# A stack of four cross-attention layers: output product in rounded halves, operands in fewer buffers, another order of jobs

## The chip, the core and the metric

The kernel runs on one core of a Trainium2 chip. The metric is the device time of one execution in microseconds (us), as the median of several runs. Five engines work side by side, each through its own instructions in order: TensorE (PE, its weight loads shown as PEld), VectorE (DVE), ScalarE (ACT), GpSimd (POOL) and SyncE (SP, which here only issues transfers). They meet through semaphores. TensorE writes to eight accumulation banks (PSUM) of 512 fp32 columns each.

## What is computed

Sixteen batches of x (100 rows by 256) go through four layers against a context of 361 rows by 256 each. The two narrow layers (L0 first, L3 last) have 16 heads of width 16; L0 ends in a feed-forward part of width 1024. The two wide layers (L1, L2) have 16 heads of width 64, so their queries, keys and values are 1024 wide. The wide part, cut to what matters:

```python
q = split_heads(norm(x) @ wq)        # 256 -> 16 heads of 64
k, v = split_heads(ctx @ wk), split_heads(ctx @ wv)
if layer == "L2": q, k = rope(q), rope(k)
attn = softmax(q @ k.T)
x = x + (attn @ v).reshape(100, 1024) @ wo     # the O product
if layer == "L2": x = layer_norm(x)
```

Everything is fp32.

## The kernel before

`build` runs four blocks, one after the other, each with a program for every engine and a barrier between: `narrow_layer("L0")`, `feed_forward`, `wide_layers` (L1 for the 16 batches, then L2 for the same 16: 32 sequences s, NS = 32, B = 16), `narrow_layer("L3")`.

**Rounded halves.** Most products do not multiply fp32 by fp32. Each operand is split in a high half (ACT copies it to the type f32r, which rounds) and a low half (DVE takes source minus high half), and `product3` (L1316) issues for each pair of operands three matmuls, high x high, high x low, low x high, into one bank. Exceptions in the wide layers are the transposes, the product with V and the **O product** (`project`, L1370 to L1381): eight fp32 matmuls of 100 weight columns by 256 columns. The trace shows an fp32 matmul that is no transpose as two rows.

**Wide layers.** A sequence is worked in four slots d = 0 to 3, each with two pairs of heads. `jobs_at(s, d)` (L1192) lists the side jobs of a slot, in three groups; every engine walks the same lists. A job takes one of three banks in turn (`begin`), and so waits until the third job before it has been taken out of its bank (`taken`). Jobs are: K, two per slot, for the next sequence; V, six per sequence (0 to 5), each 128 or 105 context rows by 512; Q and X (queries and the transpose of x, for two sequences together); R, twice per sequence, which spreads the inverse softmax sums of eight heads over partitions; O, once. TensorE's slot is: two `scores`, two `weigh` of the slot before, the jobs `first` (K, K), `turn` (six transposes), the jobs `mid` (R, V, O), `turn`, the jobs `late` (Q, X).

In L2 the keys and queries are rotated as well: DVE shuffles the result in its bank (`shuffle`, L1622), ACT then copies it out (`copy_turn`, L1482), which frees the bank, POOL multiplies (`rotate`, L1856, L1857), DVE adds (`join`, L1627), ACT rounds (L1490), DVE (K, L1633) or POOL (Q, L1863) makes the low half. For each sequence of L2 POOL also makes tables from the mask (L1837 to L1841). The scores get one matmul pair more (L1398).

After the weighing of eight heads, ACT copies R's result to OT (`spread`, L1513), DVE multiplies it by the weighed sums (`scale`, L1682) and so frees the bank PO for the next eight heads; O follows when both halves of OT are there, and DVE adds its result to X (`finish`, L1688).

**Contexts** come from memory through one raw buffer C and are split into three slots (s % 3) of CTH2 and CTL2, at d = 1, two sequences ahead (L1469, L1609). **Weights** come through W_RAW, three buffers of 1 MB; 15 chunks are split (`split_high` L1461, `split_low` L1604). SP's order at the start of the wide layers:

```python
load_output_weights(sp, "L1")
...
sp.wait_ge(Z["w_low"], 7)
load_weights(sp, "L2")
for s in range(NS):
    if s + 1 < NS:
        sp.wait_ge(Z["c_low"], KE * (s + 1))
        load_turned_context(sp, s + 1)
```

The L2 chunks are split at the ends of slots in sequences 13 to 15 (`CHUNKS_AT`), after the jobs `late`. The closing norm of L2 (`post_stats`, `post`) stands at the ends of d = 2 and d = 3.

**Narrow layers.** Before the slots stands a list FIRST: W jobs (biases, 16 matmuls of one column each, twice), context turns, K, X, Q, V. K's strips go out to memory and come back in another layout (`strips`) before scores can use them. Matmul rows with these lines: L369 (K, Q), L394 (W), L424 (V), L509 (scores), L521 (`turn`).

## Time and profile before

| | us |
|---|---|
| median of 3 runs (lowest, highest) | 2072.18 (2070.36, 2076.41) |
| profiled execution, its own time | 2078.45 |
| its span in the trace | 2076.5 |
| PE busy | 1940.1 (93%) |
| PEld busy | 1669.4 (80%) |
| DVE busy | 1383.3 (67%) |
| ACT busy | 1290.3 (62%) |
| POOL busy | 602.2 (29%) |
| mean granted TensorE clock | 0.975 |

The profiled execution has 2.0 us outside its span and is 6.3 us above the median of the runs. Reading the trace by stages: L0 runs until about 357 us, the feed-forward part until 448, L1 until about 1092, L2 until 1740, L3 until the end. Busy shares are averages over these stages, and they differ from one to the next; matmuls are pipelined and their ends are modelled, so what one costs is read from start to start. A clock of 1.00 is 2.4 GHz and one of 0.50 is 1.2 GHz.

### The profile page before, as it was taken

How to read it: one execution, taken by the hardware profiler on the slowest of the kernel's cores; microseconds unless marked ns; L12 is line 12 of the kernel's file. 1: busy time of each engine (PE TensorE's matmuls, PEld its weight loads, DVE VectorE, ACT ScalarE, POOL GpSimd, SP SyncE). 2: the span in 40 equal slices, each digit the busy share in tenths (PEclk: the TensorE clock that was granted, in tenths of full speed). 3: DMA queues.
4: the chain of work that ended last, by engine and by line, in shares of the span. 5: the costliest groups of instructions: out<-in, count | busy, mean ns of one | idle time of the engine just before them, and what ended most of it. 6: DMA issues, size and time to landing. Idle time of an engine off the chain costs nothing. (4 is left out here: it accounts for less than half of the span.)

```text
span 2076.5 us, 49737 instructions
## 1 busy us (share of the span) xinstructions
PE 1940.1 (93%) x18664; PEld 1669.4 (80%) x18664; DVE 1383.3 (67%) x2711; ACT 1290.3 (62%) x3125; POOL 602.2 (29%) x740
## 2 busy tenths in 40 slices
PE   6899997988999999999999999999999998899997
PEld 5777775986888888888888888888888877777776
DVE  5777875554555545555577888888878874677774
ACT  3677775655556555555666666666666653677775
POOL 3223230000000000000047766866776751000000
PEclk9999998999999999999999999999999998999998
DMA  5544442102000000000001000000000001434441
GB/s 163 154 129 141 135 127 80 62 23 83 8 16 9 10 14 8 16 9 9 15 2 52 10 16 10 10 13 14 10 10 17 2 1 54 124 114 130 128 130 54
DMA packets 72853, 109.56 MB, mean 53 GB/s; under 512 B 7052, under 2 KB 62508, under 8 KB 72620
## 3 DMA queue, kind: packets, MB, share of 16 engines
q1 hardware_dynamic: 72332, 105.88, 16.9%
q8 instruction: 154, 2.52, 0.5%
q14 instruction: 79, 0.65, 0.1%
q10 hardware_dynamic: 288, 0.51, 0.1%
HBM read 69.18 MB, written 37.19 MB: 51 GB/s over the span
## 5 line engine op out<-in xcount | busy, mean ns | idle before, releaser
L1533 ACT ACTIVATE wide_P<-PS,MX 100x361 f32<-100x361 f32 x512 | 280.8, 562 | 178.6 <-DVE MX L1660 178.6
L623 ACT ACTIVATE L_P<-PS,MX 100x361 f32<-100x361 f32 x512 | 252.7, 565 | 121.5 <-DVE MX L753 121.3
L753 DVE TENSOR_REDUCE MX<-PS 100x2 f32<-100x722 f32 x256 | 219.9, 901 | 49.3 <-PE PS L509 49.0
L1660 DVE TENSOR_REDUCE MX<-PS 100x2 f32<-100x722 f32 x256 | 221.3, 901 | 26.7 <-PE PS L1401 26.3
L521 PE MATMUL PP<-CON,L_P 100*128 100x100 f32 x1536 | 185.9, 259 | 25.8 <-DVE L_PT L760 17.0
L521 PEld LDWEIGHTS PP<-CON,L_P 100*128 100x128 f32 x1536 | 153.2, 145 | 47.7 <-ACT L_P L623 33.4
L1408 PEld LDWEIGHTS PS<-CON,wide_P 100*128 100x128 f32 x1536 | 159.7, 140 | 24.1 <-ACT wide_P L1533 3.0
L1408 PE MATMUL PS<-CON,wide_P 100*128 100x100 f32 x1536 | 175.5, 249 | 1.4 <-ACT wide_P L1533 1.2
L1856 POOL TENSOR_TENSOR wide_AC<-wide_T,wide_COSM 128x362 f32<-128x362 f32 x128 | 130.0, 1016 | 154.2 <-ACT wide_T L1482 148.6
L1507 ACT ACTIVATE wide_V<-PJ 128x512 f32<-128x512 f32 (+1 forms) x126 | 75.3, 598 | 145.2 <-PE PJ L1321 143.3
L1421 PEld LDWEIGHTS PP<-wide_PT,wide_V 128*64 128x64 f32 (+1 forms) x3072 | 136.0, 136 | 32.5 <-issue 32.5
L1421 PE MATMUL PP<-wide_PT,wide_V 128*64 128x100 f32 (+1 forms) x3072 | 161.2, 253 | 0.1
L1816 POOL TENSOR_TENSOR VE<-MV 128x2 f32<-128x2 f32 x8 | 1.7, 218 | 505.8 <-DVE MV L1713 505.8
L1321 PE MATMUL PJ<-wide_CTH,wide_WH 128*128 128x362 f32 x336 | 120.7, 359 | 15.6 <-DVE wide_CTL L1609 9.5
L1857 POOL TENSOR_TENSOR wide_SH<-wide_SH,wide_SINM 128x362 f32<-128x362 f32 x128 | 132.5, 1036 | 0.0
L1321 PE MATMUL PJ<-wide_WH,wide_CTH 128*128 128x512 f32 (+1 forms) x252 | 107.5, 427 | 12.1 <-ACT wide_T L1482 11.2
L1321 PE MATMUL PJ<-wide_CTH,wide_WL 128*128 128x362 f32 x336 | 111.5, 332 | 0.0
L1321 PE MATMUL PJ<-wide_CTL,wide_WH 128*128 128x362 f32 x336 | 111.3, 331 | 0.0
L760 DVE COPY L_PT<-PP 128x600 f32<-128x600 f32 x128 | 99.5, 777 | 13.4 <-PE PP L521 9.0
L1533 ACT ACTIVATION_READ_ACCUMULATOR wide_P<-PS,MX 100x1 f32 x512 | 103.8, 203 | 0.0
L1633 DVE TENSOR_TENSOR wide_KL<-wide_AC,wide_KH 128x362 fp32r<-128x362 f32 x128 | 102.9, 844 | 0.0
L1666 DVE COPY wide_PT<-PS 128x600 f32<-128x600 f32 x128 | 99.1, 774 | 2.3 <-PE PS L1408 2.3
(242 smaller groups left out, 5369.5 us busy)
## 6 DMA issues: line engine op xcount, KB each, us to landing
strips<-L_KS SPq DMA_DIRECT2D x256, 90.5 KB
L_KA<-strips SPq DMA_DIRECT2D x64, 362.0 KB, 3.1
C<-ctx_t SPq DMA_DIRECT2D x32, 361.0 KB, 3.1
kept<-L_CTH SPq DMA_DIRECT2D x16, 361.0 KB, 4.6
kept<-L_CTL SPq DMA_DIRECT2D x16, 361.0 KB, 5.5
L_CTH<-kept SPq DMA_DIRECT2D x16, 361.0 KB, 4.2
L_CTL<-kept SPq DMA_DIRECT2D x16, 361.0 KB, 5.2
C<-in_ctx SPq DMA_DIRECT2D x8, 256.0 KB, 3.4
```

Of the source, the lines that this page charges most:

```text
L521: last = nc.tensor.transpose(PPB[:, n, SQ * t:SQ * t + SQ], P[:, (4 * g + 2 * i + n) % 8, 128 * t:128 * t + 128], ident[0:SQ, 0:SQ])
L623: nc.scalar.activation(P[:, (4 * g + j) % 8, 0:SK], PSB[0:SQ, j, 0:SK], ACT.Exp, bias=MX[:, s % 2, 4 * q + j:4 * q + j + 1], scale=1.0).th ...
L753: nc.vector.tensor_reduce(MX[:, s % 2, 4 * q + 2 * i:4 * q + 2 * i + 2], PSB[0:SQ, 2 * i:2 * i + 2, 0:SK], AX.X, ALU.max, negate=True).the ...
L760: nc.vector.tensor_copy(pt(g)[:, 2 * KV_TILES * SQ:4 * KV_TILES * SQ].rearrange("p (n c) -> p n c", n=2), PPB[:, :, 0:KV_TILES * SQ]).then ...
L1321: last = nc.tensor.matmul(dst, l, r, start=n == 0, stop=n == len(todo) - 1)
L1408: last = nc.tensor.transpose(score_bank(g, i)[:, SQ * t:SQ * t + SQ], P[:, (2 * g + i) % 4, 128 * t:128 * t + 128], ident[0:SQ, 0:SQ])
L1421: last = nc.tensor.matmul(PO[64 * i:64 * i + 64, SQ * at:SQ * at + SQ], V[0:r, 1024 * c + 64 * h:1024 * c + 64 * h + 64], PT[0:r, (2 * g + ...
L1533: nc.scalar.activation(P[:, (2 * g + i) % 4, 0:SK], score_bank(g, i)[0:SQ, 0:SK], ACT.Exp, bias=MX[:, s % 2, h:h + 1], scale=1.0, accum_ou ...
L1633: nc.vector.tensor_tensor(KL[:, p, :], AC[:, r % NB, 0:SKE], KH[:, p, :].bitcast(fp32), ALU.subtract).then_inc(Z["k_low"], 1)
L1660: nc.vector.tensor_reduce(MX[:, s % 2, 2 * p:2 * p + 2], PSB[0:SQ, 2 * (g % 2):2 * (g % 2) + 2, 0:SK], AX.X, ALU.max, negate=True).then_in ...
L1856: nc.gpsimd.tensor_tensor(ac, src, c, ALU.mult)
L1857: nc.gpsimd.tensor_tensor(sh, sh, t, ALU.mult).then_inc(Z["rotated"], 1)
```

## The change

1. **O product.** `project` becomes a `product3` over eight pairs: 24 f32r matmuls instead of 8 fp32 ones. OT gives way to a buffer RB of half its size and the halves OTH and OTL. ACT rounds RB (`output_high`, at the ends of d = 2 and of the next d = 0), DVE subtracts (`output_low`, in d = 3 and the next d = 1, behind the maxima): 64 new instructions on each. The weights are split too (`output_weights_high`, `_low`): four chunks of 1024 columns, two of them in L1's slot (0, 1), one each in (16, 3) and (17, 0).
2. **Space.** Contexts in two slots (s % 2), split at d = 3 instead of d = 1. W_RAW has two buffers; a third and WO lie in `shared`, which is given back before the wide layers, where WOL and WOH take its place.
3. **Loads.** SP loads the context of sequence 1 ahead of the L2 weights; Wq and Wv of L2 come then, Wk at s = 14.
4. **Order in the wide layers.** V before R in d = 0 and d = 2; V(s + 1, 0) moves from d = 2 to d = 3. Chunks are split ahead of `mid` instead of behind `late`. `post_stats` and `post` move to d = 1, the latter by a whole sequence.
5. **Order in the narrow layers.** FIRST has K, X, K before the second W; K(1, 0) moves into slot (0, 0).
6. **Fillers.** `keep_busy` issues fp32 matmuls of 128 columns whose result nobody reads: 12 in FIRST of L0, 4 in each of the six slots from (15, 1) to (16, 2) of both narrow layers, 9 at L0's end, 12, 7 and 8 in the feed-forward part, 9 at the start and 4 and 14 at the end of the wide layers.

The diff, cut to its core (indices of DVE's and ACT's job lists that follow FIRST, and s % 3 to s % 2 in the readers, are left out):

```diff
-        W_RAW = sb("W_RAW", [128, 3, 2048])
-        WO = sb("WO", [128, 2048])
+        W_RAW = sb("W_RAW", [128, 2, 2048])
...
+        def keep_busy(dst, n):
+
+            for _ in range(n):
+                nc.tensor.matmul(dst[:, 0:128], ident, CON[:, 0:128], start=True, stop=True)
+
...
+        shared = ExitStack()
+        WO = shared.enter_context(nc.sbuf_tensor("WO", [128, 2048], fp32))
+        W_RAW_Q = shared.enter_context(nc.sbuf_tensor("W_RAW_Q", [128, 2048], fp32))
+
         def raw(c, n):
-            return W_RAW[:, c, 0:KE * n].rearrange("p (k n) -> p k n", k=KE)
+            if c == 2:
+                at = W_RAW[:, 1, 1024:1024 + KE * n] if n == E else W_RAW_Q[:, 0:KE * n]
+            else:
+                at = W_RAW[:, c, 0:KE * n]
+            return at.rearrange("p (k n) -> p k n", k=KE)
...
+                    if s == 0:
+                        b_.append(("K", 1, 0))
...
-            FIRST = ([("W", 0, 0)] + ctx0 + [("W", 0, 1), ("K", 0, 0), ("K", 0, 1), ("X", 0, 0)] + [("Q", 0, t) for t in range(4)]
-                     + [("V", 0, 0), ("V", 0, 1)] + ctx1 + [("K", 1, 0)])
-            lead = len(ctx0) + 5
+            FIRST = ([("W", 0, 0)] + ctx0 + [("K", 0, 0), ("X", 0, 0), ("K", 0, 1), ("W", 0, 1)] + [("Q", 0, t) for t in range(4)]
+                     + ctx1 + [("V", 0, 0), ("V", 0, 1)])
...
                     strips(0, 0)
-                    strips(0, 1)
                     if first:
                         sp.wait_ge(Z["c_normed"], 2)
                         load_context(sp, 3, CS[1], s_c[1])
+                    strips(0, 1)
+                    if first:
+                        keep(0)
                     strips(1, 0)
                     if first:
-                        keep(0)
                         keep(1)
...
-                    for key in FIRST:
+                        keep_busy(PSB[:, 3, :], 6)
+                    for n, key in enumerate(FIRST):
                         job(key)
+                        if first and n in (0, KE):
+                            keep_busy(PSB[:, 3, :], 4 if n == 0 else 2)
...
+                        if (B - 1, 1) <= (s, q) <= (B, 2):
+                            keep_busy(begin(("P" if q == 0 else jobs_at(s, q + 1)[0][0][0], s - 1, 0) if q < 3 else ("O", s - 1, 0)), 4)
+                    keep_busy(PSB[:, 3, :], 9 if first else 0)
...
+                    keep_busy(PSB[:, 3, :], 12)
                     for k in range(KE):
                         turn(0, k)
+                    keep_busy(PSB[:, 3, :], 7)
...
+                    keep_busy(PSB[:, 3, :], 8)
...
+            WOL, WOH = local("WOL", [128, 2048], f32r), local("WOH", [128, 2048], f32r)
             WH, WL = local("WH", [128, 6144], f32r), local("WL", [128, 6144], f32r)
-            CTH2, CTL2 = local("CTH", [128, 3, KE, SKE], f32r), local("CTL", [128, 3, KE, SKE], f32r)
...
-            OT = local("OT", [128, 8, SQ])
+            RB = local("RB", [128, 4, SQ])
+            OTH, OTL = local("OTH", [128, 8, SQ], f32r), local("OTL", [128, 8, SQ], f32r)
+            WO_HALVES = [slice(1024 * n, 1024 * n + 1024) for n in range(2)]
+            WO_AT = {(0, 1): [0, 1], (B, 3): [2], (B + 1, 0): [3]}
             Y = XN[:, 0, :]
...
+                if d == 0 and 0 < s < NS:
+                    mid.append(("V", s, 2))
                 if d == 0 and s > 0:
                     mid.append(("R", s - 1, 1))
-                if d == 0 and 0 < s < NS:
-                    mid.append(("V", s, 2))
                 if d == 1 and s > 0:
                     mid.append(("O", s - 1, 0))
+                if d < 3 and s < NS:
+                    mid.append(("V", s, 3 + d))
                 if d == 2 and s < NS:
                     mid.append(("R", s, 0))
-                if d < 3 and s < NS:
-                    mid.append(("V", s, 3 + d))
-                if d >= 2 and s + 1 < NS:
-                    mid.append(("V", s + 1, d - 2))
+                if d == 3 and s + 1 < NS:
+                    mid += [("V", s + 1, 0), ("V", s + 1, 1)]
...
+                    def weights(m):
+                        sp.dma_start(W_RAW[:, RAW2[m], :].rearrange("p (k n) -> p k n", k=KE),
+                                     a["L2_xattn_W" + m.lower()].rearrange("(k p) n -> p k n", p=128)).then_inc(w_in["L2"]["KVQ".index(m)], 16)
+
                     load_output_weights(sp, "L1")
                     sp.wait_ge(Z["padded"], 1)
                     mask(B)
                     mask(B + 1)
-                    sp.wait_ge(Z["w_low"], 7)
-                    load_weights(sp, "L2")
                     for s in range(NS):
                         if s + 1 < NS:
                             sp.wait_ge(Z["c_low"], KE * (s + 1))
                             load_turned_context(sp, s + 1)
+                        if s == 0:
+                            sp.wait_ge(Z["w_low"], 7)
+                            for m in "QV":
+                                weights(m)
+                        if s == B - 2:
+                            sp.wait_ge(Z["w_low"], 9)
+                            weights("K")
...
-                        pe.wait_ge(Z["scaled"], 2 * (s + 1))
-                        if s == 0:
-                            pe.wait_ge(wo_in["L1"], 16)
-                        if s == B:
-                            pe.wait_ge(wo2_in, 16)
-                        dst = begin(key)
-                        for t in range(8):
-                            last = nc.tensor.matmul(dst[0:SQ, 0:E], OT[:, t, :], WO[:, E * t:E * t + E], start=t == 0, stop=t == 7)
-                        last.then_inc(Z["made"], 1)
+                        pe.wait_ge(Z["o_low"], 2 * (s + 1))
+                        pe.wait_ge(Z["wo_low"], 2 if s < B else 4)
+                        product3(begin(key)[0:SQ, 0:E], [(OTH[:, t, :], OTL[:, t, :], WOH[:, E * t:E * t + E], WOL[:, E * t:E * t + E]) for t in range(8)])
...
+                    keep_busy(PSB[:, 0, :], 9)
                     pe.wait_ge(Z["padded"], 1)
...
+                        if s == NS:
+                            keep_busy(PSB[:, 0, :], 4 if d == 0 else 14)
...
-                            if s >= 3:
-                                act.wait_ge(Z["made"], job_no["V", s - 3, 5] + 1)
-                        nc.scalar.activation(CTH2[:, s % 3, k, 0:SK], ctx_raw(s)[:, k, :], ACT.Copy).then_inc(Z["c_high"], 1)
+                            if s >= 2:
+                                act.wait_ge(Z["made"], job_no["V", s - 2, 5] + 1)
+                        nc.scalar.activation(CTH2[:, s % 2, k, 0:SK], ctx_raw(s)[:, k, :], ACT.Copy).then_inc(Z["c_high"], 1)
...
+                        if 2 * s + r:
+                            act.wait_ge(Z["o_low"], 2 * s + r)
+                        nc.scalar.activation(RB[:, :, :].rearrange("p t q -> p (t q)"), bank(key)[:, 0:4 * SQ], ACT.Copy).then_inc(Z["spread"], 1)
+
+                    def output_high(s, r):
+                        act.wait_ge(Z["scaled"], 2 * s + r + 1)
+                        if s:
+                            act.wait_ge(Z["made"], job_no["O", s - 1, 0] + 1)
+                        nc.scalar.activation(OTH[:, 4 * r:4 * r + 4, :], RB[:, :, :], ACT.Copy).then_inc(Z["o_high"], 1)
+
+                    def output_weights_high(n):
+                        if n < 2:
+                            act.wait_ge(wo_in["L1"], 16)
+                            act.wait_ge(Z["w_low"], 7)
+                        else:
+                            act.wait_ge(wo2_in, 16)
+                            act.wait_ge(Z["made"], job_no["O", B - 1, 0] + 1)
+                        h = WO_HALVES[n % 2]
+                        nc.scalar.activation(WOH[:, h], WO[:, h], ACT.Copy).then_inc(Z["wo_high"], 1)
...
-                        if d == 1 and s + 2 < NS:
+                        if d == 3 and s + 2 < NS:
                             for k in range(KE):
                                 context_high(s + 2, k)
+                        for c in CHUNKS_AT.get((s, d), ()):
+                            split_high(c)
+                        for n in WO_AT.get((s, d), ()):
+                            output_weights_high(n)
                         for key in mid:
                             job(key)
                         if s < NS:
                             unload(2 * G + 1)
                         for key in late:
                             job(key)
-                        for c in CHUNKS_AT.get((s, d), ()):
-                            split_high(c)
+                        if d == 0 and s:
+                            output_high(s - 1, 1)
+                        if d == 2 and s < NS:
+                            output_high(s, 0)
...
-                        o = OT[:, 4 * r:4 * r + 4, :].rearrange("p t q -> p (t q)")
+                        o = RB[:, :, :].rearrange("p t q -> p (t q)")
                         nc.vector.tensor_tensor(o, PO[:, 0:4 * SQ], o, ALU.mult).then_inc(Z["scaled"], 1)
+
+                    def output_low(s, r):
+                        dve.wait_ge(Z["o_high"], 2 * s + r + 1)
+                        t = slice(4 * r, 4 * r + 4)
+                        nc.vector.tensor_tensor(OTL[:, t, :], RB[:, :, :], OTH[:, t, :].bitcast(fp32), ALU.subtract).then_inc(Z["o_low"], 1)
+
+                    def output_weights_low(n):
+                        dve.wait_ge(Z["wo_high"], n + 1)
+                        h = WO_HALVES[n % 2]
+                        nc.vector.tensor_tensor(WOL[:, h], WO[:, h], WOH[:, h].bitcast(fp32), ALU.subtract).then_inc(Z["wo_low"], 1)
...
+                        if d == 1 and s:
+                            output_low(s - 1, 1)
+                        if d == 3 and s < NS:
+                            output_low(s, 0)
...
-                        if d == 1 and s + 2 < NS:
+                        if d == 1 and B + 2 <= s <= NS:
+                            post(s - 2)
+                        if d == 3 and s + 2 < NS:
                             for k in range(KE):
                                 context_low(s + 2, k)
+                        for c in CHUNKS_AT.get((s, d), ()):
+                            split_low(c)
+                        for n in WO_AT.get((s, d), ()):
+                            output_weights_low(n)
                         for key in mid:
                             job(key)
...
-                        if B < s < NS:
-                            if d == 2:
-                                post_stats(s - 1)
-                            if d == 3:
-                                post(s - 1)
+                        if B < s < NS and d == 1:
+                            post_stats(s - 1)
...
+                shared.close()
                 wide_layers()
+                WO = sb("WO3", [128, KE * E])
```

## Rows read from the trace of the kernel before

**Rows 1.** Stages: us, busy time of each engine (instructions), granted clock, DMA share, GB/s
```profile
357.00:371.00 14.00, 6.25 (x23) 5.93 (x24) 10.58 (x22) 7.84 (x9) 2.16 (x2) 0.51 0.74 266
440.00:520.00 80.00, 62.75 (x468) 56.28 (x466) 41.64 (x87) 41.25 (x98) 3.64 (x8) 0.89 0.20 68
560.00:1010.00 450.00, 448.87 (x3850) 390.40 (x3850) 228.65 (x428) 257.82 (x693) 6.61 (x20) 1.00 0.04 11
1136.00:1662.00 526.00, 510.70 (x4440) 444.81 (x4439) 432.85 (x902) 337.56 (x916) 378.66 (x442) 1.00 0.04 11
1740.00:1785.00 45.00, 36.52 (x205) 32.51 (x206) 23.02 (x47) 19.28 (x40) 4.33 (x10) 0.70 0.37 114
```

**Rows 2.** TensorE's waits: who waited for whom, us in total, times, longest
```profile
PE PJ L1321 <- ACT wide_T L1482: 11.2, 10, 1.5
PE PJ L1321 <- DVE wide_CTL L1609: 9.5, 1, 9.5
```

**Rows 3.** Timeline of TensorE, starts of sequences 2, 14, 17 and 30 (start, duration)
```profile
556.03 0.41 PE L1401 MATMUL PS<-wide_KH,wide_QH 64*100 64x362 f32 x2
...
1012.16 0.41 PE L1401 MATMUL PS<-wide_KH,wide_QH 64*100 64x362 f32 x2
...
1135.95 0.41 PE L1398 MATMUL PS<-wide_MNEG,wide_FILL 64*100 64x362 f32 x2
...
1662.81 0.41 PE L1398 MATMUL PS<-wide_MNEG,wide_FILL 64*100 64x362 f32 x2
```

**Rows 4.** Timeline of TensorE: an O product and what follows; f32r matmuls of 256 columns
```profile
570.54 3.62 PE L1380 MATMUL PJ<-WO,wide_OT 128*100 128x256 f32 x16
573.81 0.58 PE L1321 MATMUL PJ<-wide_WH,wide_CTH 128*128 128x512 f32 x1
574.23 0.40 PE L1321 MATMUL PJ<-wide_WL,wide_CTH 128*128 128x512 f32 x1
574.47 0.39 PE L1321 MATMUL PJ<-wide_WH,wide_CTL 128*128 128x512 f32 x1
...
321.11 0.28 PE L424 MATMUL PJ<-L_WH,L_CTH 128*128 128x256 f32 x1
321.23 0.28 PE L424 MATMUL PJ<-L_WL,L_CTH 128*128 128x256 f32 x1
```

**Rows 5.** Timeline of TensorE in L2: the same 512-column job at either clock, and a stall
```profile
1101.05 0.69 PE L1321 MATMUL PP<-wide_WH,wide_CTH 128*105 128x512 f32 x1 [1.69 <-ACT wide_T L1482]
1101.54 0.63 PE L1321 MATMUL PP<-wide_WL,wide_CTH 128*105 128x512 f32 x1
1101.96 0.63 PE L1321 MATMUL PP<-wide_WH,wide_CTL 128*105 128x512 f32 x1
...
1075.76 0.41 PE L1321 MATMUL PJ<-wide_CTH,wide_WH 128*128 128x362 f32 x1 [1.49 <-issue]
```

**Rows 6.** Timeline of DVE, POOL and TensorE early in sequence 20
```profile
1257.92 0.89 DVE L1702 SCALAR_TENSOR_TENSOR X<-wide_XN,RS,ROWS 100x256 f32<-100x256 f32 x1
...
1268.42 0.54 POOL L1863 TENSOR_TENSOR wide_QL<-wide_AC,wide_QH 128x200 fp32r<-128x200 f32 x1
...
1269.07 0.41 PE L1398 MATMUL PS<-wide_MNEG,wide_FILL 64*100 64x362 f32 x2 [0.26 <-issue]
```

**Rows 7.** Durations of one, ns: min/median/max, first and last start
```profile
L1513 ACT ACTIVATE wide_OT<-PJ x44: 489/500/532, 506.1 to 1724.2; 128x400 f32<-128x400 f32 x44
...
L1609 DVE TENSOR_TENSOR wide_CTL<-C,wide_CTH x64: 503/530/1302, 449.8 to 1642.6; 128x361 fp32r<-128x361 f32 x64
...
L1633 DVE TENSOR_TENSOR wide_KL<-wide_AC,wide_KH x128: 518/818/1312, 1067.2 to 1709.0; 128x362 fp32r<-128x362 f32 x128
```

**Rows 8.** Timeline of TensorE at the starts of L3 and L0
```profile
1742.56 3.37 PE L394 MATMUL PJ<-VEC,W_RAW 128*128 128x1 f32 x16 [4.91 <-POOL L_CTL L891]
...
1764.75 0.41 PE L509 MATMUL PS<-L_KA,L_QA 32*100 32x362 f32 x4
...
36.42 0.41 PE L509 MATMUL PS<-L_KA,L_QA 32*100 32x362 f32 x4
```

34 lines of the change are left out of this document (16 added, 18 removed).

## Prediction

> **What bounds it now.** I began with the busy time by stage [rows 1]. In L1 (560 to 1010 us) TensorE is busy for 448.9 of 450.0 us at full clock, with DVE at 51% and ACT at 57%: nothing but TensorE's own work counts there. In L2 (1136 to 1662) it is still busy for 97%, but DVE is at 82%, POOL at 72%, ACT at 64%, and the missing 15 us are waits. The edges between stages differ again: the clock is 0.51 at the start of the feed-forward part and 0.89 where L1 begins. Second, TensorE's waits [rows 2]: one of 9.5 us for the context of sequence 1, and ten, 11.2 us together, for ACT's copy of a K result out of one of two banks. Third, the starts of sequences [rows 3]: L1 takes (1012.16 - 556.03) / 12 = 38.01 us per sequence, L2 (1662.81 - 1135.95) / 13 = 40.53. L2 has eight more pairs of score matmuls per sequence; one step of a 362-column matmul is some 0.17 us (362/512 of the 512-column step of 0.24 [rows 4]), so its floor is 38.0 + 1.3 = 39.3 and 1.2 us per sequence are waits. Between sequences 14 and 17 lie 123.8 us where 2 x 38.0 + 39.3 = 115.3 were due: 8.5 us are lost around the change of layer.
>
> **O product.** Before: 16 rows from 570.54, the next job at 573.81, whose second matmul comes 0.42 later where the third takes 0.24, so 0.19 of that is still the O product: 3.27 + 0.19 = 3.46 us, or 0.216 per row [rows 4]. After: 24 f32r matmuls of 256 columns. The nearest rows are the V matmuls of the narrow layers, also 256 columns and with 128 weight columns, one every 0.12 us [rows 4]: 24 x 0.119 = 2.86 us. That is 0.60 less per sequence, and as TensorE is the bound in both layers, 32 x 0.60 = **-19.2 us**. Bounds: 0.107 a step if only the columns counted (-29), 0.130 with the stretching that jobs next to others show (-11); I take the even spacing. What is new beside it: on ACT 64 roundings of 128x400, 0.50 each like OT's copies [rows 7], 1 us per sequence on an engine with 16 free; on DVE 64 subtractions. In L1 one takes about 0.55 and is hidden in 19 free us per sequence.
>
> In L2 the price on DVE is less sure. Subtractions of two SBUF operands take 0.52 at best and 1.31 at worst, with a median of 0.82 for K's [rows 7]; the long ones stand beside POOL's work. The Trainium skill ("SBUF — State Buffer", section "SBUF: two separate sides") says that DVE with two SBUF inputs and a reading GpSimd exclude each other for whole instructions, a rule that speaks against putting two more such instructions into L2; the trace agrees with it in kind. I take 0.9 each from the rows: DVE goes from 33.4 to 35.2 us of some 39 per sequence, still below TensorE.
>
> The split of WO in slot (0, 1) costs ACT 2 us and DVE 2.4 us in a slot where both are half idle: nothing. The two chunks in (16, 3) and (17, 0), 1.3 us of DVE each, fall into L2's fuller slots: +1. At the very end O waits for one more pass through ACT and DVE: +1.2.
>
> **Context of sequence 1.** SP waits for the seventh chunk and then puts 3 MB ahead of it. Now it goes as soon as the first context is split, some 25 us before it is needed. The 9.51 us go, and with them the low clock that the idle time brought about (the stretch 440 to 520 has 0.89) and that TensorE worked at for 4.5 us more, half of it lost for one us and more. Taken as **-10.5 us**. SP's later loads are early enough: Wk leaves at s = 14, once the Q chunks are split, 30 us before its first chunk is taken. Two context slots instead of three cost nothing as long as the split at d = 3 (1 us of ACT, 1.1 to 2.6 of DVE) is done before K at the next d = 0, about 7 us later.
>
> **L2's waits for a bank.** In d = 0 the order is K, K, turn, R, V2; V2 takes K0's bank, and K0 is late since DVE comes late to its shuffle, behind the closing norm of the sequence before (0.89 us at 1257.92), the maxima, the inverse sums and three joins [rows 6]. Two edits meet here: with V2 ahead of R, V2 takes the bank of the slot before, and 1.4 us of work cover the wait; and the norm is gone from that place. The waits of 1.5 and 0.8 us at d = 0 should vanish. What is late next: POOL. Its row at 1268.42 makes the low half of a query which the scores at 1269.07 wait for, and POOL works through the tables and rotations ahead of it without a break, so this wait of 0.5 us in even sequences can grow to 1 us when TensorE arrives sooner. And d = 3 now holds, for DVE, the context, an output half and no norm, nearly 10 us of work in a slot that grows from 8 to 9.4 us by V's move. Of the 16 x 1.2 = 19 us I take **-12**; bounds -19 and +3.
>
> **Change of layer.** The chunks at slot ends delay the next maxima: TensorE stood 1.49 us before a K at 1075.76, and 1.69 us at 1101.05, after which the first eight 512-column matmuls ran at 1.2 GHz, 0.42 apart instead of 0.24 [rows 4, 5]. Ahead of `mid` they lie in slack. Of 8.5 us, 1.2 already counted: **-4.5**, between -7 and 0.
>
> **Narrow layers' starts.** L3's W jobs take 3.4 us each for 16 one-column matmuls at the low clock, and the first scores come at 1764.75; in L0 at 36.42 [rows 8]. The new order lets K0 start one W earlier, takes a K job (1.0 us at full clock) out of the way of the first scores, and the fillers should bring the full clock sooner. L3: fetch of the kept context holds K0 until about 1746.5, then X, K, W, four Q (0.7 each), two V: first scores near 1758, with K(1, 0) behind them: -5 with full clock, -2 without; I take -4. L0 by the same count from 16 us on: first scores near 29 to 30 with one K less: -5.5, between -8 and -2. In both, strips' round trips start earlier as well, so that the gain is kept.
>
> **Fillers.** 123 matmuls of half of O's columns, fp32 as they are: 2 x 0.108 = 0.216 us each, 26.6 us in all, 0.43 each at the low clock. Those in waits are free. Not free are those ahead of a barrier: 9 at L0's end (1.9 us, of which DVE's last addition hides 0.5) and 8 at the end of the feed-forward part (0.7 beyond DVE); 14 at the wide end are hidden by the closing norm's 3.2 us. In return the feed-forward part and L1 begin at full clock: the clock was 0.51 over 357 to 371, with 6.3 us of matmul work in it [rows 1]. Taken as -1 for both boundaries and -2 for the two tails, where chains of turns and unloads run at the low clock in part. Bounds +6 and -8.
>
> **Sum** against the profiled execution (2078.45): -19.2 - 10.5 - 12 - 4.5 + 1 + 1.2 - 4 - 5.5 - 3 = -56.5, so 2022. The median lies 6.3 below that execution, and I expect the changed kernel's median by the same step: 2072.2 - 56.5 = 2015.7. I say **2016 us**, with 2003 to 2029 as this case's own range (0.6).
>
> **Rivals.**
> - *L2 keeps its waits.* DVE and POOL set its pace: d = 3 overflows, each output half costs 1.3, the bank waits turn into waits for low halves. For: DVE at 82%, POOL's row at 1268.42 [rows 6]. Against: 4 us per sequence remain free on DVE. L2 then gives 0 instead of -12 and the change of layer -2: 2030, at worst 2040. Chance 0.18.
> - *The edges give nothing.* The fillers do not hold the clock and the starts are bound by transfers: -12.5 becomes +3: 2031. Chance 0.1.
> - *All waits go*, and the clock stays full: L2 -18, edges -22, layer -7: 1998. Chance 0.07.
> - *Slower: weight loads show.* O has 24 weight loads instead of 16. If none were hidden behind the matmul before, a step would be load plus columns; with the load rows of the old O product at 0.167 us and the step of 0.119 that gives 24 x 0.286 = 6.9 us instead of 3.46: 32 x 3.4 = +109, hence 2016 + 19 + 109 = 2144. It decides from a step of 0.144 on, where 24 of them equal the old 3.46. Against it: the narrow V matmuls, each with its own weights, are 0.12 apart with loads of over 0.16 [rows 4]. Chance 0.02. The Trainium skill ("TensorE: Matmul & The Clock Gate", section "The mechanism") has it that a weight load overlaps running matmuls only for another row group, which would expose every load here; the trace does not agree.
> - *O's product is no cheaper* (100-column weights step at 0.144): 2035. Chance 0.03.
>
> **How the numbers follow.** About 0.3% is what a measurement of this kernel can tell from no change. Only the weight loads give a slower kernel, 0.03 with what I overlooked; within 0.3% needs several terms to fail together, 0.02; faster 0.95. The range must take in the two rivals near 2030 and their worst ends and most of the fast one: 1997 to 2041.
>
> **What would show it.** O: 24 rows 0.12 apart and V's next matmul 2.9 us after O's first. L1 at 37.4 us per sequence, L2 at 39.2 or so (38.7 is its floor). The 9.5 us wait gone, the ACT wait on L1482 down from 11.2 to a few us, a wait for POOL's L1863 grown. First scores at 1764.75 less all that went before less 4. I am wrong if L2 stays above 40, if L1 doesn't fall by 0.6, or if the first scores of L0 come after 34.

## Result, and the profile after

The changed kernel takes 2038.8 us (median of four runs, 2034.64 to 2039.82) against 2073.2 (four runs, 2070.36 to 2076.41): a ratio of 0.983, with a 95% interval of 0.981 to 0.985. That is 34 us less where 56 were forecast: inside the range given (1997 to 2041), outside the case's own range (2003 to 2029). The profiled execution took 2039.82 us with a span of 2038.0, where before it was 2076.5.

The page of the changed kernel, its head and one row of its slices:

```profile
span 2038.0 us, 51007 instructions
PE 1936.0 (95%) x19166; PEld 1683.5 (83%) x19166; DVE 1433.7 (70%) x2779; ACT 1312.6 (64%) x3193; POOL 642.4 (32%) x740
...
PEclk8899999999999999999999999999999998999999
```

By stage, to be read beside [rows 1] (columns as there: the stretch, busy us of each engine, granted clock, DMA):

```profile
340.00:360.00 20.00, 17.67 (x245) 14.90 (x235) 7.83 (x14) 7.88 (x16) 0.00 (x0) 1.00 0.01 2
560.00:990.00 430.00, 430.00 (x3863) 383.18 (x3862) 237.53 (x443) 258.36 (x700) 11.67 (x20) 1.00 0.04 11
1136.00:1610.00 474.00, 463.74 (x4138) 405.23 (x4137) 414.75 (x849) 316.96 (x865) 369.32 (x402) 1.00 0.05 12
```

L1 has no idle time, as before. In L2 DVE is now busy for 414.8 of 474 us, 88% where it was 82%, and POOL for 369.3, 78% where it was 72%, though it executes the same 740 instructions over the whole run. TensorE's waits, beside [rows 2]:

```profile
PE PP L536 <- DVE L_PT L781: 23.1, 20, 9.3
...
PE PJ L1405 <- ACT wide_T L1516: 4.5, 4, 1.1
...
PE PP L1405 <- ACT wide_T L1516: 3.9, 4, 1.1
PE PS L1429 <- issue: 3.8, 8, 0.5
...
PE PS L1429 <- POOL wide_QL L1935: 2.6, 1, 2.6
```

The waits of the two old lines are gone, the 9.5 us for the context of sequence 1 among them. In their place stand a wait of up to 9.3 us in L0 (L536), one of 1.1 us ahead of R (L1405) in the even sequences 16 to 28 of L2, and in the same ones one of 0.5 us ahead of the scores of the second pair in d = 1 (L1429). These scores come right after POOL's low half of a query has ended, as in sequence 20:

```profile
1243.22 0.53 POOL L1935 TENSOR_TENSOR wide_QL<-wide_AC,wide_QH 128x200 fp32r<-128x200 f32 x1
...
1243.86 0.41 PE L1429 MATMUL PS<-wide_MNEG,wide_FILL 64*100 64x362 f32 x2 [0.53 <-issue]
```

The starts of sequences 2, 14, 17 and 30 answer to [rows 3], and the O product with V's matmul behind it to [rows 4], in TensorE's timeline:

```profile
546.83 0.41 PE L1432 MATMUL PS<-wide_KH,wide_QH 64*100 64x362 f32 x2
...
561.20 0.34 PE L1358 MATMUL PJ<-wide_WOH,wide_OTH 128*100 128x256 f32 x1
561.38 0.28 PE L1358 MATMUL PJ<-wide_WOL,wide_OTH 128*100 128x256 f32 x1
561.50 0.28 PE L1358 MATMUL PJ<-wide_WOH,wide_OTL 128*100 128x256 f32 x1
...
564.11 0.40 PE L1358 MATMUL PJ<-wide_WH,wide_CTH 128*128 128x512 f32 x1
564.35 0.40 PE L1358 MATMUL PJ<-wide_WL,wide_CTH 128*128 128x512 f32 x1
...
992.85 0.41 PE L1432 MATMUL PS<-wide_KH,wide_QH 64*100 64x362 f32 x2
...
1110.79 0.41 PE L1429 MATMUL PS<-wide_MNEG,wide_FILL 64*100 64x362 f32 x2
...
1630.87 0.41 PE L1429 MATMUL PS<-wide_MNEG,wide_FILL 64*100 64x362 f32 x2
```

The steps are 0.12 us, and O now takes 564.11 - 561.20 = 2.91 us; V's second matmul comes the usual 0.24 later. From such starts the 38.5 us between the two spans can be laid out. The middle column puts the terms of the prediction into the same stretches, with 0.60 for each O in it:

```
stretch (first scores to first scores)         before    predicted   measured
up to sequence 0 of the wide layers            474.8       -7.5        +2.4
wide 0 to 2                                     81.2      -11.1       -11.6
L1, 2 to 14                                    456.1       -7.2       -10.1
change of layer, 14 to 17                      123.8       -6.1        -5.9
L2, 17 to 30                                   526.9      -17.5        -6.8
30 to the first scores of L3                   101.9       -6.1        -3.3
L3 and its tail                                311.7       -1          -3.2
```

The start of L1 and the change of layer came as forecast, L1 brought 3 us more; what is missing is up to the wide layers (10 us) and in L2 (11 us). The first of these lies in L0: its first scores come 2.5 us earlier than before, those of sequence 4 come 1.8 later and those of sequence 15 come 4.3 later; from there to the wide layers 1.9 us are won, near the 2 that were forecast. Nine of the traces have the same code up to sequence 0 of the wide layers and reach it between 473.8 and 479.9 us, 476.7 in the mean; so the 2.4 in the table is within their spread, and the missing 10 are not.

### The profile page after: what moved, and what is told of

Read it like the earlier page. It is cut to its first block and busy times, and to the rows that moved or that the text cites. A ratio compares the mean times of both kernels' runs of the same rounds, so it can differ in the third digit from the quotient of the medians.

```text
span 2038.0 us, 51007 instructions
## 1 busy us (share of the span) xinstructions
PE 1936.0 (95%) x19166; PEld 1683.5 (83%) x19166; DVE 1433.7 (70%) x2779; ACT 1312.6 (64%) x3193; POOL 642.4 (32%) x740
## 5 line engine op out<-in xcount | busy, mean ns | idle before, releaser
L536 PE MATMUL PP<-CON,L_P 100*128 100x100 f32 x1536 | 181.6, 255 | 27.6 <-DVE L_PT L781 23.1
L536 PEld LDWEIGHTS PP<-CON,L_P 100*128 100x128 f32 x1536 | 149.2, 143 | 48.8 <-ACT L_P L644 34.8
L1452 PEld LDWEIGHTS PP<-wide_PT,wide_V 128*64 128x64 f32 (+1 forms) x3072 | 136.1, 136 | 33.1 <-issue 33.1
L1929 POOL TENSOR_TENSOR wide_SH<-wide_SH,wide_SINM 128x362 f32<-128x362 f32 x128 | 138.3, 1080 | 0.0
L1690 DVE TENSOR_TENSOR wide_KL<-wide_AC,wide_KH 128x362 fp32r<-128x362 f32 x128 | 114.2, 932 | 0.0
L1516 ACT ACTIVATE wide_T<-PJ 128x362 f32<-128x362 f32 (+1 forms) x128 | 54.6, 427 | 74.7 <-DVE wide_SH L1679 72.8
```

Of the source, the lines that this page charges most:

```text
L536: last = nc.tensor.transpose(PPB[:, n, SQ * t:SQ * t + SQ], P[:, (4 * g + 2 * i + n) % 8, 128 * t:128 * t + 128], ident[0:SQ, 0:SQ])
L1452: last = nc.tensor.matmul(PO[64 * i:64 * i + 64, SQ * at:SQ * at + SQ], V[0:r, 1024 * c + 64 * h:1024 * c + 64 * h + 64], PT[0:r, (2 * g + ...
L1690: nc.vector.tensor_tensor(KL[:, p, :], AC[:, r % NB, 0:SKE], KH[:, p, :].bitcast(fp32), ALU.subtract).then_inc(Z["k_low"], 1)
L1929: nc.gpsimd.tensor_tensor(sh, sh, t, ALU.mult).then_inc(Z["rotated"], 1)
```

## The experiments

Twelve kernels ran, in groups of four, four, three and one. Each has its ratio to the kernel before, measured beside it on the same chip; the changed kernel's is 0.983. Slots of L2 are compared by their mean length over sequences 18 to 29, from the first score matmul of a slot to that of the next, in even and odd sequences apart:

```
              even d0    d1     d2     d3  | odd d0    d1     d2     d3  | per sequence, 17 to 30
before         11.48  11.89   9.71   8.00 |  10.74  11.43   9.71   8.30 | 40.53
b_v2           10.58  12.82   9.71   8.00 |   9.86  11.44   9.72   8.29 | 40.14
o_fp32         11.58  12.21   8.34   9.47 |  10.11  11.43   8.34   9.75 | 40.52
changed        11.55  11.62   8.35   9.50 |  10.08  10.79   8.34   9.77 | 40.01
out_low        10.84  11.62   8.35   9.44 |   9.75  10.82   8.34   9.73 | 39.44
ctx_low         9.78  12.24   8.35   9.48 |   9.88  10.79   8.34   9.75 | 39.36
pool_order     11.73  10.84   8.34   9.73 |  10.29  10.81   8.34  10.01 | 40.52
ctx_spread     10.05  12.25   8.34  10.11 |   9.74  10.82   8.34  10.43 | 40.07
rx_act         11.52  11.62   8.34   9.80 |  10.49  10.79   8.33  10.11 | 40.54
rx_pool        11.24  10.86   8.35   9.80 |  10.50  10.79   8.33  10.10 | 40.07
rx_pool_ctx    10.48  10.85   8.34  10.18 |   9.77  10.81   8.33  10.49 | 39.74
pool_ctx_l0    10.06  10.86   8.35  10.11 |   9.74  10.81   8.34  10.42 | 39.45
```

The shortest of each slot with the new O product (9.74, 10.79, 8.33, 9.44) make 38.3 us, an estimate of L2 without waits. Each row is one profiled execution. How far such a row repeats is shown by l0_order and no_fill (below), whose wide layers are those of the changed kernel (no_fill lacks the fillers at their start and end): both have 40.02 per sequence, and none of their slots is more than 0.04 from the changed kernel's. L1 was 38.01 before, 37.95 in b_v2, 37.79 in o_fp32 and 37.17 in all others.

### The O product put back: o_fp32

```diff
-product3(begin(key)[0:SQ, 0:E], [(OTH[:, t, :], OTL[:, t, :], WOH[...], WOL[...]) for t in range(8)])
+for t in range(8):
+    last = nc.tensor.matmul(dst[0:SQ, 0:E], OT[:, t, :], WO[:, E * t:E * t + E], start=t == 0, stop=t == 7)
```

> The changed kernel with the O product of the wide layers put back: sixteen fp32 matmuls from the unsplit OT and WO, and with that the 64 roundings, the 64 subtractions and the four WO chunks are gone too; everything else of the change stays. Step of the prediction (the O product is worth 0.60 us per sequence in both layers): L1 goes from 37.17 to 37.8 us per sequence, L2 from 40.0 to 40.6, the whole to 2038.8 + 19 = 2058. Rival 1 (the rest of the change slowed L1's slots, the product itself gives more): L1 goes to 38.0, as it was before, +10 us for L1 alone. Rival 2 (in L2 the two output halves on DVE eat what the product gives): L2 stays at 40.0 or falls below it, and the whole ends near 2048.

Measured: 2060.2 us, ratio 0.9925 (0.991 to 0.994). L1 37.79 us per sequence, so the product gives 0.62 there, and the rest of the change another 0.22, which I had at nothing. (From the rows of one O product alone it is 3.46 - 2.91 = 0.55.) L2 40.52, 0.51 above the changed kernel; the sum from sequence 0 to 30 is 15.5 us. The step of the prediction holds in size. And L2 without the new O product is where it was before the change: everything else in it adds up to nothing there.

### V2 ahead of R, alone: b_v2

```diff
-if d == 0 and s > 0:        mid.append(("R", s - 1, 1))
 if d == 0 and 0 < s < NS:   mid.append(("V", s, 2))
+if d == 0 and s > 0:        mid.append(("R", s - 1, 1))
```

> The kernel before with one part of the change alone: at d = 0 of the wide layers V's third piece stands ahead of R. By the prediction the 1.4 us of V2's matmuls on the bank of the slot before cover the wait for K0's bank: of the 11.2 us of waits for the copy of K0 some 8 go, L2 falls from 40.53 to 40.0 us per sequence and the whole by 6 to 8 us. Rival (R then takes K0's bank and waits in V2's place, as the 1.1 us stops ahead of R in the changed kernel suggest): L2 stays within 0.15 of 40.53, the whole within 2 us of 2073.

Measured: 2066.5 us, ratio 0.996 (0.9946 to 0.9975), L2 down by 0.39 us per sequence, 1.9 more at the change of layer. The order is worth what I had expected of it in the kernel before. The slots show how: d = 0 falls by 0.9 in even and in odd sequences; in odd ones it is kept, in even ones d = 1 grows by 0.93. There the wait ahead of the scores is now as large as the old bank waits; in TensorE's waits of b_v2 (in the kernel before, the even d = 1 waits of this kind came to 0.2 us each):

```profile
PE PS L1398 <- issue: 8.0, 7, 1.2
```

So in the changed kernel something took back this order's 0.39, too. Of the 5.1 us at the change of layer (123.8 to 118.7 in o_fp32), 1.9 come with this order alone.

### DVE's new work in L2: out_low and ctx_low

```diff
+t, q = slice(4 * r, 4 * r + 4), slice(0, SQ if s < B else 1)          # out_low
+nc.vector.tensor_tensor(OTL[:, t, q], RB[:, :, q], OTH[:, t, q].bitcast(fp32), ALU.subtract)
+q = slice(0, SK if s < B + 3 else 4)                                  # ctx_low
+nc.vector.tensor_tensor(CTL2[:, s % 2, k, q], ctx_raw(s)[:, k, q], CTH2[:, s % 2, k, q].bitcast(fp32), ALU.subtract)
```

> The changed kernel, with the two subtractions for O's low half cut to one of 100 columns in each of the four blocks, in L2 alone (most of the low half of L2's O inputs is left out); all waits stay. Theory A (DVE is late in L2 since d = 3 now holds the context, an output half and the evictions' partners): about 1.1 us of DVE per sequence go, and L2 falls by 0.3 to 0.6 us per sequence, the whole by 4 to 8 us. Theory B (the order of V2 and R and the move of V cost it, whatever DVE does): L2 stays at 40.0 within 0.1. Theory C (POOL is the late one): POOL's busy time falls by under 10 us, and the stops at d = 1 for the low half of a query stay at 0.5 us or more.

> The changed kernel, with the subtraction for the low half of the contexts cut to 4 of its columns in L2, from its fourth context on (that low half is left out); all waits stay. 2.5 us of DVE go from each d = 3 of even and odd sequences. Theory A (DVE at d = 3 hands its lateness to the next d = 0): the d = 0 slots of even sequences fall from 11.55 to 10.3 us or less, L2 by 0.6 us per sequence or more, the whole by 7 to 12 us. Theory B (order of V2 and R): they stay at 11.5. Theory C (POOL): d = 0 falls a little, and d = 1 stays at 11.6 or rises, since TensorE comes sooner to the same late low half.

Measured: out_low 2034.6 us, ratio 0.9806 (0.979 to 0.982), L2 39.44; ctx_low 2034.4 us, ratio 0.980 (0.978 to 0.983), L2 39.36. Each takes 0.6 us per sequence off L2, 7.4 and 8.4 us between sequences 17 and 30, so it is DVE's work, and the order of V2 and R is not to blame. The times of the whole say less: 4 us by the medians, with ratios whose intervals overlap the changed kernel's. In ctx_low d = 0 of even sequences is at its floor, and d = 1 grows by 0.6, as theory C had it: POOL is next in line.

But DVE's load alone is not the measure: o_fp32 takes both output halves from DVE altogether and leaves d = 0 as it was. The timelines around d = 3 of sequence 19 tell why. First POOL in the changed kernel:

```profile
1223.03 0.54 POOL L1935 TENSOR_TENSOR wide_QL<-wide_AC,wide_QH 128x200 fp32r<-128x200 f32 x1
1223.53 2.19 POOL L1928 TENSOR_TENSOR wide_AC<-wide_T,CON 128x200 f32<-128x200 f32 x1
1225.67 0.54 POOL L1929 TENSOR_TENSOR wide_SH<-wide_SH,CON 128x200 f32<-128x200 f32 x1
```

DVE in the same kernel and place:

```profile
1223.78 0.56 DVE L1744 TENSOR_TENSOR wide_OTL<-wide_RB,wide_OTH 128x400 fp32r<-128x400 f32 x1
1224.27 0.97 DVE L1684 TENSOR_TENSOR wide_AC<-wide_AC,wide_SH 128x362 f32<-128x362 f32 x2
1226.25 0.37 DVE L1684 TENSOR_TENSOR wide_AC<-wide_AC,wide_SH 128x200 f32<-128x200 f32 x1 [1.01 <-POOL wide_SH L1929]
```

And POOL in out_low, the same two instructions of the same slot:

```profile
1221.01 0.61 POOL L1928 TENSOR_TENSOR wide_AC<-wide_T,CON 128x200 f32<-128x200 f32 x1
1221.58 1.35 POOL L1929 TENSOR_TENSOR wide_SH<-wide_SH,CON 128x200 f32<-128x200 f32 x1
```

POOL's multiplication takes 0.61 us by itself and 2.19 where DVE works through the output half and two joins, which end at 1225.24: it gets on only when they are through. The third join then waits 1.01 us for POOL, and with it all that DVE does up to the maxima of the next d = 0. With a short output half the third join starts 0.76 us earlier in its slot, near the 0.71 of d = 0. In o_fp32 the same stretching hits POOL's low half instead (2.1 us), one instruction earlier. It is so in every d = 3 from sequence 17 to 29, in the mean:

```
               third join, us    its wait     longest POOL instruction
               from slot start   for POOL     in the slot's first 4 us
before, b_v2        4.29           0.00       0.72  a multiplication
changed             5.18           1.01       2.19  a multiplication
out_low             4.42           0.43       1.35  a multiplication
o_fp32              5.20           1.51       2.12  low half of a query
rx_act (below)      5.55           1.51       2.43  low half of a query
pool_ctx_l0 (below) 5.87           0.00       2.43  a step of the norm, one column
```

So whether DVE has an output half or not, its third join begins at 5.2 us, since POOL is caught at another of its instructions. The Trainium skill ("SBUF — State Buffer", section "SBUF: two separate sides") has such an instruction of DVE, with two inputs from SBUF, and one of GpSimd that reads SBUF shut each other out for the whole instruction. The rows agree in kind. They don't show that whoever starts first goes first: POOL's row starts 0.25 us ahead of DVE's output half, and it is POOL that waits (spans on POOL are rough). The mask's step on POOL shows it as well (ns, shortest, median and longest of one; L1841 of the kernel before took 1128, 1274 and 1489), in the changed kernel:

```profile
L1913 POOL TENSOR_SCALAR wide_MNEG<-wide_MNEG x12: 1473/1978/2485, 1156.5 to 1599.5; 128x362 fp32r<-128x362 f32 x12
```

and in pool_ctx_l0, where it stands at another place:

```profile
L1924 POOL TENSOR_SCALAR wide_MNEG<-wide_MNEG x12: 1135/1136/1142, 1164.7 to 1597.6; 128x362 fp32r<-128x362 f32 x12
```

The stretching doesn't vanish there, it falls on another instruction. A one-column step of the norm on POOL, in the changed kernel and in pool_ctx_l0:

```profile
L1899 POOL TENSOR_SCALAR EV<-MV x12: 219/226/229, 1146.1 to 1587.8; 128x1 f32<-128x1 f32 x12
...
L1906 POOL TENSOR_SCALAR EV<-MV x12: 2422/2432/2439, 1143.6 to 1577.2; 128x1 f32<-128x1 f32 x12
```

How full is the pair? At their shortest durations, POOL has per sequence of L2 16 multiplications of 0.82, eight of 0.53 to 0.60, four low halves of 0.53, 3.3 for the tables and 0.8 for the norm: 23.8 us. DVE's instructions with two inputs from SBUF are 8 joins and 8 low halves of 0.52, four joins of 0.35, two of contexts at 0.54, two of outputs at 0.56, and 2.0 for the norm: 13.9. Together that is 37.7 of 40.0 us, if none can run beside one of the other. This sum is an estimate and was not tested. It leaves out the copy that repeats the inverse sums, which has a single input from SBUF and took 0.43 to 1.03 us in L2 of the changed kernel.

### Moves on POOL and DVE: pool_order, ctx_spread, rx_act, rx_pool, rx_pool_ctx

```diff
 # pool_order, POOL at d == 0                      # ctx_spread, ACT and DVE, L2 only
+for key in keys[:1]: rotate(key)                   +d == 2, at its end: context_high/low(s + 2, 0)
+rotated_low of the query                           +d == 3: k = 1 alone
+for key in keys[1:]: rotate(key)
+d == 2, at its end: less_one(s + 1)
 # rx_act: the copy RX <- RDEN goes from DVE's invert to ACT, behind the four exponentials
```

> The changed kernel with two moves on POOL in L2: at d = 0 the low half of a query goes between the two rotations of K instead of behind them, and the step that takes one off the mask (1.1 to 2.5 us, 16 times) goes from d = 0, ahead of the rotations, to d = 2. Theory A (DVE's lateness makes d = 0 late, POOL's low half of a query makes d = 1 of even sequences late): d = 1 of even sequences falls from 11.62 to 10.8 or 10.9 and d = 0 stays at 11.5, L2 falls by 0.4 us per sequence, the whole by 5 us. Theory B (POOL alone is the bound, d = 0 included, since the joins wait for its rotations): d = 0 falls too, by 0.5 us or more, and the whole by 8 us or more. Theory C (POOL is not what scores wait for): nothing changes.

Measured: 2042.4 us, ratio 0.9865 (0.984 to 0.989), L2 40.52: 3.6 us slower than the changed kernel by the medians, with intervals that overlap. Even d = 1 went to 10.84 as in theory A, but d = 0 and d = 3 of all sequences grew by 0.2 each, which gives the 0.78 back. The rest, some 6 us, is one stop in sequence 17 that I had made myself. SP asks for L2's WO only behind a load that waits for the mask's step, which now comes two slots later, and ACT stands for it:

```profile
1114.04 1.06 ACT L1565 ACTIVATE wide_WOH<-WO 128x1024 fp32r<-128x1024 f32 x1 [4.62 <-DMA WO<-in_L_xattn_Wo]
```

> The changed kernel with one move in L2: of the two pieces of a context, the first is split at the end of d = 2, on ACT and DVE, and only the second at d = 3. Theory A (DVE's work at d = 3 is what makes the next d = 0 late; ctx_low, with both pieces cut, took that slot from 11.55 to 9.78): half of that comes without leaving anything out, so d = 0 of even sequences falls to 10.3 to 10.9, d = 1 grows by 0.3 (POOL is late next), L2 falls by 0.3 to 0.4 us per sequence and the whole by 4 to 5 us. Rival (the piece makes d = 3's maxima late instead): d = 2 plus d = 3 grow by as much as d = 0 falls, and the whole stays within 1 us.

Measured: 2037.5 us, ratio 0.984 (0.981 to 0.986), L2 40.07. d = 0 fell by 1.5 and 0.34, d = 1 of even sequences grew by 0.63 and each d = 3 by 0.6: the rival. Either lateness alone, taken away, reappears one or three slots later.

> The changed kernel with one instruction moved from DVE to ACT in both wide layers: the copy that repeats the inverse sums (1.03 us, twice per sequence, at d = 0 and d = 2). Nothing else differs. Theory A (DVE's load sets L2's waits; it is 88% busy there and its work at d = 0 stands ahead of the shuffle of K0): d = 0 of even sequences falls from 11.55 to 10.5 to 10.9, d = 1 rises by up to 0.6 (POOL is late next), L2 falls by 0.3 to 0.6 us per sequence, the whole by 4 to 8 us; L1 stays at 37.17. Rival (ACT becomes late instead, since its exponentials and copies are in the same chain): L2 stays within 0.1 of 40.0 or rises.

> As rx_act, and on POOL the low half of a query goes between the two rotations of K at d = 0, the mask's step of minus one to the end of POOL's work in the same d = 0. Theory A (two causes in a row: DVE at d = 0, then POOL's low half at d = 1): d = 0 of even sequences as in rx_act, d = 1 at 10.8 to 10.9, so L2 another 0.3 to 0.7 us per sequence lower, at 39.0 to 39.3, the whole at 2022 to 2028. Rival (POOL's instructions at another time only stretch DVE's beside them, as where minus one went to d = 2, which gave back at d = 0 and d = 3 what d = 1 had won): L2 within 0.1 of rx_act.

> As rx_pool, and the first piece of each context of L2 is split at the end of d = 2 instead of at d = 3. Alone that move took 1.5 us from d = 0 of even sequences and 0.34 from odd ones, and gave it all back: 0.63 at d = 1 (POOL late) and 0.6 at each d = 3. Theory A (the part given back at d = 1 is POOL's, and with POOL mended it stays won; that at d = 3 is DVE's, and with 1 us less ahead of it at d = 2 it shrinks to 0.3): L2 at 38.7 to 39.0. Rival (DVE's work only moves, and with rx_act d = 0 has no lateness left to win): L2 0.2 to 0.5 us per sequence above rx_pool.

Measured: rx_act 2045.0 us, ratio 0.985 (0.983 to 0.987), L2 40.54; rx_pool 2037.0, 0.981 (0.9795 to 0.983), L2 40.07; rx_pool_ctx 2030.7, 0.979 (0.977 to 0.981), L2 39.74. Theory A fell for rx_act: a microsecond less on DVE left d = 0 of even sequences where it was and cost 0.3 to 0.4 at d = 3 and at odd d = 0, where TensorE now waits for ACT's copies (in the code the copy on ACT waits for the reciprocal, with K's and Q's behind it). In the table above, DVE's output half now catches POOL at the low half of a query, as in o_fp32, and the third join waits 1.51 us. The other two levels were missed as well: rx_pool was to reach 39.0 to 39.3 and came to 40.07, rx_pool_ctx 38.7 to 39.0 and came to 39.74. The steps have the signs of theory A, not of the rivals: 0.47 less for the new place on POOL, where the rival said 0.1 at most, and 0.33 less for the context's, where the rival said 0.2 to 0.5 more. The new place on POOL (the mask's step last in the same d = 0) keeps its 0.76 at d = 1 and gives nothing back, and with it ctx_spread's move pays as well. The low half and the mask's step were moved together each time; which of them brings the 0.76 was not taken apart.

### Loads at L0's start: l0_order

```diff
+sp.wait_ge(Z["c_normed"], 3)
+load_context(sp, 4, CS[0], s_c[0])
 for s in range(B):
+    if first and s == 2: ... load_weights(sp, "ffn")
```

The stop, in DVE's timeline of the changed kernel:

```profile
67.13 0.43 DVE L787 BATCH_NORM_STATS2 BN<-C 128x6 f32<-128x256 f32 x1 [9.32 <-DMA C<-in_ctx]
```

and SP's queue ahead of it, where the strips of sequence 1 go out at 51.53 and come back at 62.95 only, before the context can be asked for:

```profile
51.53 2.39 SPq L302 DMA_DIRECT2D strips<-L_KS  x4
62.95 0.33 SPq L307 DMA_DIRECT2D L_KA<-strips  x1
63.32 0.43 SPq L131 DMA_DIRECT2D C<-in_ctx  x1
```

> The changed kernel with another order of loads on SP in L0: the fifth context (s = 4) is asked for before the round trip of the strips of sequence 1, second half, and the feed-forward weights two sequences later. Theory A (L0's start is bound by SP, which stands in the strips' round trips and reaches that context's load at 63.3 us only, so that DVE waits 9.3 us for it): the stop goes, sequences 0 to 2 of L0 take 42 us or less instead of 48.8, and the whole falls by 5 to 9 us. Theory B (the transfers themselves are the bound, the DMA engines being busy): the stop only moves to the strips or to the next context, and sequences 0 to 4 take as long as before within 2 us.

Measured: 2036.7 us, ratio 0.9835 (0.981 to 0.986): nothing. Sequences 0 to 2 took 36.8 us instead of 48.8, more than theory A asked for; 9.8 of these 12.0 us were lost in the next two sequences, and 2.1 ahead of sequence 0, whose first scores came that much later. The stops in DVE's timeline of l0_order:

```profile
80.69 0.43 DVE L790 BATCH_NORM_STATS2 BN<-L_C 128x6 f32<-128x256 f32 x1 [1.86 <-DMA L_C<-in_ctx]
...
105.23 0.43 DVE L790 BATCH_NORM_STATS2 BN<-C 128x6 f32<-128x256 f32 x1 [5.63 <-DMA C<-in_ctx]
```

SP's queue of l0_order suggests what bounds the start: a round trip of the strips starts every 9 to 10 us, two per sequence, and while SP stands for the strips to land it sends nothing else.

```profile
60.48 3.87 SPq L302 DMA_DIRECT2D strips<-L_KS  x4
...
69.46 2.17 SPq L302 DMA_DIRECT2D strips<-L_KS  x4
...
79.41 4.01 SPq L302 DMA_DIRECT2D strips<-L_KS  x4
...
89.70 2.66 SPq L302 DMA_DIRECT2D strips<-L_KS  x4
```

The first scores of L0's sequence 4 come at 119.3 us in the kernel before, 121.1 in the changed one, 120.9 in l0_order and 120.5 in pool_ctx_l0, though those of sequence 0 lie between 33.3 and 36.4. So theory A had the stop right and theory B what comes of it: sequences 0 to 4 take 84.9 us instead of 87.1, and moving one load in SP's queue only moves the stop. Whether SP's standing or the slowness of the transfers themselves (in l0_order the DMA engines are busy for 47 to 54% between 15 and 105 us) makes a round trip so long was not taken apart; a start in which SP doesn't stand in the round trips was not tried. Past the start it is not what bounds L0: from 120 to 320 us SP stands for the strips 105.7 us in the changed kernel, and TensorE is busy for 189.2 of the 200.

### No fillers: no_fill

```diff
-for _ in range(n):
+for _ in range(0):
     nc.tensor.matmul(dst[:, 0:128], ident, CON[:, 0:128], start=True, stop=True)
```

> The changed kernel without its 123 fillers; nothing else differs. Step of the prediction (they bring the full clock sooner and are worth some 3 us in all, with 2 to 3 more at the two starts): the whole rises from 2038.8 to 2042 to 2045, with low granted clock over the change of layer's end and L3's start. Rival 1 (the gaps that they fill are few and their own time ahead of barriers costs as much): within 2 us of 2039. Rival 2 (the clock falls in many places, as before the change, where some 105 us were at the low level): 2050 or more.

Measured: 2042.0 us, ratio 0.9857 (0.983 to 0.988). That is 3 us by the medians and 6 by the ratios, and the intervals overlap, so more than "a few us" can't be said. The fillers do what they are for at L0's end and in the feed-forward part. The stretch 320 to 370 us, changed kernel:

```profile
320.00:370.00 50.00, 41.17 (x594) 34.65 (x594) 28.15 (x50) 26.14 (x49) 2.16 (x2) 1.00 0.20 58
```

and no_fill:

```profile
320.00:370.00 50.00, 32.88 (x437) 26.07 (x436) 27.47 (x49) 26.92 (x49) 2.16 (x2) 0.79 0.22 73
```

The clock is granted in full instead of 0.79. In the traces no_fill loses 2.1 us from L0's sequence 15 to the wide layers, 3.2 from sequence 30 to L3, 2.5 in L3 with its tail, and wins 2.0 in L0. Kernels of the same code there differ by as much: the way from sequence 30 to L3 takes 98.6 us in the changed kernel and 102.3 in l0_order, and over the eleven with fillers it takes 96.7 to 102.7.

At L0's start the fillers bring the full clock, but don't hold it. In no_fill the 200-column matmuls of Q come 0.21 us apart there, all at the low clock, and the first scores at 35.5 us. In the changed kernel the clock is granted in full from 17.7 us on and these matmuls come 0.11 apart; it falls at 24.5, while TensorE waits 1.29 us for DVE, and stays at 0.50 until 34.7, past the first scores at 34.0:

```profile
23.46 0.28 PE L384 MATMUL PJ<-L_XTL,L_WH 128*128 128x200 f32 x1
23.57 0.27 PE L384 MATMUL PJ<-L_XTH,L_WL 128*128 128x200 f32 x1
25.14 0.51 PE L384 MATMUL PJ<-L_XTH,L_WH 128*128 128x200 f32 x1 [1.29 <-DVE L_QB L722]
25.44 0.41 PE L384 MATMUL PJ<-L_XTL,L_WH 128*128 128x200 f32 x1
25.66 0.41 PE L384 MATMUL PJ<-L_XTH,L_WL 128*128 128x200 f32 x1
```

TensorE is busy for 9.1 of these 10.2 us at half its clock, which is some 4.5 us of the way to the first scores (an estimate from these figures).

### Both moves and L0's order: pool_ctx_l0

> The changed kernel with the moves that won something, and without the one that did not (repeating the inverse sums stays on DVE): on POOL the low half of a query between the two rotations of K and minus one at the end of the same d = 0; the first piece of each context of L2 split at the end of d = 2; SP's order of loads in L0 as in l0_order. Theory A (lateness of DVE at d = 0 and of POOL at d = 1 stand in a row, and either alone only hands it on): d = 0 of even sequences at 10.0 to 10.3 us, d = 1 at 10.85, d = 3 at 10.1 and 10.4, L2 at 39.2 to 39.5 us per sequence; the first scores of the wide part 3 us earlier by L0; the whole at 2024 to 2029, ratio 0.977 to 0.979, so faster than both kernels. Rival (a sum of load on DVE and POOL, not places, bounds L2): L2 at 39.7 or above, the whole at 2031 or above.

Measured: 2028.0 us (five runs, 2023.95 to 2032.62), ratio 0.978 (0.976 to 0.980), whose interval lies below the changed kernel's: faster than both. Every slot is where theory A had it, and L2 at 39.45. The start of the wide part came 0.4 us earlier, not 3. Its page, and the start of sequences 17 and 30:

```profile
span 2026.4 us, 51007 instructions
PE 1937.0 (96%) x19166; PEld 1689.3 (83%) x19166; DVE 1434.1 (71%) x2779; ACT 1313.2 (65%) x3193; POOL 670.7 (33%) x740
```

```profile
1109.61 0.41 PE L1432 MATMUL PS<-wide_MNEG,wide_FILL 64*100 64x362 f32 x2
...
1622.43 0.41 PE L1432 MATMUL PS<-wide_MNEG,wide_FILL 64*100 64x362 f32 x2
```

DVE is as busy as in the changed kernel (1434 us) and POOL busier by 28, yet L2 is 7 us shorter. So it is not the sum of their work but the places where they meet. Of the 10.8 us between the two medians these 7.3 are L2's; the rest lies behind it, in the way to L3 and in L3, where kernels of the same code differ by as much. POOL's two moves are in it as one, so the share of each stays open.

## Why the prediction was right, and where it was wrong

The changed kernel is faster, as forecast, and for the most part by the terms that were to make it so, but its time lies in the stated range by 2 us only: two terms of the sum failed by 10 and 11 us, both the same way, and a third repaid 3. The rival of L2 and half of that of the edges came true together, which the rivals' times, each taken by itself, had not priced.

**Right.** The O product: 0.12 us a step, 0.62 us per sequence in L1, against 0.60. The trace had no f32r matmul of 100 weight columns by 256, and the nearest row [rows 4] gave its price. No weight load shows, against what the rival feared. The rule of the Trainium skill named with it ("TensorE: Matmul & The Clock Gate", section "The mechanism": a load overlaps running matmuls only for another row group) would expose every load, 6.9 us by the prediction's figures (its load of 0.167 us stands in no row shown; it is the mean of the loads of WO in the trace of the kernel before); measured were 2.91. (The same section also lets a load go ahead into the background weight buffer, which would agree with the 2.91; the prediction left that out.) The context of sequence 1: 81.2 to 70.2 us in o_fp32, where O is unchanged, 11.0 against 10.5. The change of layer: 123.8 to 118.7 there, 5.1 against 4.5; but 1.9 of it comes with V2 ahead of R (b_v2), for which only 0.75 of L2's term was counted in this stretch, so the price of the chunks' new place was partly luck. The way to L3 and L3 itself came near what was said, within what kernels of the same code differ by; the order of jobs at L3's start has no run of its own.

**Wrong, 11 us: "Of the 16 x 1.2 = 19 us I take -12" for L2's waits.** It got nothing. The term had two parts. V2 ahead of R brings 0.39 us per sequence by itself (b_v2), in odd sequences alone, since in even ones POOL's low half takes all of it. I had named that wait and put its growth at 0.5 us; it grew by 0.93. The other part was a sentence at a price of nothing: that the context can go to d = 3. There it stands ahead of the next maxima, and without it the next d = 0 falls from 11.55 to 9.78 in even sequences (ctx_low). The 0.39 is gone again in o_fp32, where also POOL's low half at d = 3 is stretched and the third join begins at 5.20 us instead of 4.29; how much of the loss is the context's and how much this stretching's was not taken apart. The first rival had this mechanism ("d = 3 overflows", "the bank waits turn into waits for low halves") and L2 at nothing, as measured; it was given 0.18. The sign "if L2 stays above 40" came in, though barely: 40.01.

The step that failed is that of the price on DVE. I added 0.9 us for each output half to DVE's busy time and found room in the sum, 35.2 of 39. The sum came out (414.75 / 474 of 40.01 us is 35.0), and an output half took only 0.56 us; the room was not there all the same. The rule on DVE and GpSimd was cited and used as a surcharge on DVE's instruction. What it does is to hold up the other engine, whose result DVE then waits for: 1.6 us of POOL at one place, 1.01 of DVE behind it, in each sequence.

**Wrong, 10 us: L0's start, "first scores near 29 to 30", -5.5, "so that the gain is kept".** They came at 33.95 in the profiled execution, a hair under the sign at 34 (33.1 to 35.6 in the eight others with the same code there), and nothing is kept at sequence 4. Two steps failed. That the fillers bring the full clock: it was lost again from 24.5 to 34.7 us, and the some 4.5 us that this cost by the estimate above are what is missing to 29 or 30. And that the gain is kept since the strips' round trips start earlier: I didn't count them in SP's queue, where two of 7 to 11 us each stand in every sequence; l0_order shows that a load moved in this queue only moves the stop, while what makes the trips long stays open. Between sequences 4 and 15 another 2.5 us are lost; there two kernels with the same code in L0 as the changed one need 4.7 us less and 1.0 more, so it may be chance.

**Better than said, 3 us: L1.** The rest of the change gave 0.22 per sequence beside the product, 0.06 of it V2 ahead of R (b_v2). I had held that nothing but TensorE's own work counts there; where the other 0.16 is from was not taken apart.

## What to carry to other kernels

When two engines share an access, price a new instruction by what it holds up on the other engine and who waits for that, not by its own duration; busy shares of 82% and 72% may leave no room at the places where the two meet. Look there for the instruction that is stretched: the same 2.4 us cost nothing on a step that nobody waits for (pool_ctx_l0). A lateness that is taken away at one place must be followed to the next place where it can appear before its gain is booked: here another place for the context gave nothing alone, another order on POOL gave nothing with the mask's step at a bad place, and the two, with the step put right, gave 7 us in L2. At the start of a stage, count the queue that issues the transfers as an engine of its own, with its round trips.

## What was not expected of the hardware

A POOL multiplication of 128x200 took 0.61 us alone and 2.19 beside three DVE instructions in a row with two inputs from SBUF; DVE's own subtraction of 128x361 took 0.53 in L1, where POOL is nearly idle, and 1.29 in L2, beside POOL. Both directions occur, and the longest cases are on POOL: up to ten times its own length for a one-column step, 2.43 us instead of 0.23. Taking one from a mask of 128x362 takes POOL 1.13 us at best, more than multiplying two operands of that size (0.82). Writing 362 KB of strips to memory, from the first write to where the read back can be asked for, takes 7 to 11 us at L0's start, while contexts and weights are moved by the same queue; the read takes 3 us more to land.
